# An AdaLN block of gated scan, SwiGLU and routed experts: a new order of loads and work in the first stage, additions counted from one, and the last shared tile taken out of its banks first

## The reference

```
x = L0_attn_x                                    # 2 x 2048 x 512
h = layernorm(x) * (1 + ca) + sa
q, k, v = split(rms(h) @ w_qkv.T);  q, k = rms(q), rms(k)
w = exp(k)
y = sigmoid(q) * (cumsum(w * v) / (cumsum(w) + 1e-6))
u, g = split(y @ w_swiglu.T)
x = x + ga * (h + u * silu(g) @ w_out.T)
h = layernorm(x) * (1 + cb) + sb
shared = gelu(h @ shared_w1 + shared_b1) @ shared_w2 + shared_b2
routed = sum over the 2 best of 8 experts of gate * (gelu(h @ w1 + b1) @ w2 + b2)
x = x + gb * (routed + shared)
```

## Time and profile before

| | us |
|---|---|
| median of three runs | 2011.24 (2011.04 to 2012.4) |
| the profiled execution, by its own timing | 2010.7 |
| its span in the trace | 2008.9 |
| TensorE busy | 1944.8 (97%) |
| VectorE busy | 1279.0 (64%) |
| ScalarE busy | 646.6 (32%) |
| GpSimd busy | 438.7 (22%) |
| mean granted TensorE clock | 0.987 |

### The profile page before, as it was taken

The page is one execution under the profiler, slowest core; times in us unless marked ns, Lnnn a source line. Parts: engine busy times, 40 slices in busy tenths (PEclk is TensorE's granted clock), DMA queues, the critical chain, the costliest instruction groups (busy, mean ns, idle before and its releaser), DMA issues.

```text
span 2008.9 us, 26671 instructions
## 1 busy us (share of the span) xinstructions
PE 1944.8 (97%) x9106; PEld 1567.2 (78%) x9106; DVE 1279.0 (64%) x2674; ACT 646.6 (32%) x1318; POOL 438.7 (22%) x315
## 2 busy tenths in 40 slices
PE   6999999999999999998999999999999999999996
PEld 4677888888888888886887787777787667688885
DVE  6577777685545555559164465466367686488886
ACT  3545556631111112111112212212223223255553
POOL 0012000040000000017000110110052252458887
PEclk8999999999999999999999999999999999999998
DMA  5124110141011210123111311311235464468888
GB/s 224 58 89 132 51 53 27 48 142 63 24 39 63 74 44 20 63 79 121 65 63 63 107 47 67 123 65 53 96 106 179 130 199 154 146 117 152 154 154 130
DMA packets 86112, 189.99 MB, mean 95 GB/s; under 512 B 10021, under 2 KB 26662, under 8 KB 80940
## 3 DMA queue, kind: packets, MB, share of 16 engines
q1 hardware_dynamic: 63116, 130.98, 19.3%
q0 software_dynamic: 22864, 57.31, 13.8%
HBM read 118.56 MB, written 72.12 MB: 95 GB/s over the span
## 4 chain that ended last, share of the span: by engine, by line
PE 75%; DVE 14%; issue 4%; ACT 4%; DMA 2%; SPq 0%; POOLq 0%; ACTq 0%; DVEq 0%
PE bank L670 11%; PE bank L672 11%; PE bank L671 11%; PE bank L675 8%; PE bank L677 8%; PE bank L676 8%; PE bank L909 3%; PE bank L911 2%; PE bank L896 1%; PE bank L939 1%; PE bank L937 1%; PE bank L938 1%; PE bank L836 1%; PE bank L689 1%; ACT kv_sum L1084 1%
## 5 line engine op out<-in xcount | busy, mean ns | idle before, releaser
L670 PE MATMUL bank<-x_hi,w_blk 128*128 128x512 f32 x1024 | 404.0, 395 | 9.2 <-DVE x_lo L1315 6.3
L672 PE MATMUL bank<-x_hi,w_blk 128*128 128x512 f32 x1024 | 399.9, 390 | 0.0
L671 PE MATMUL bank<-x_lo,w_blk 128*128 128x512 f32 x1024 | 399.4, 390 | 0.0
L1473 DVE TENSOR_TENSOR s_t<-act_t,bank 128x512 f32<-128x512 f32 x128 | 87.8, 686 | 302.9 <-PE bank L672 300.1
L670 PEld LDWEIGHTS bank<-x_hi,w_blk 128*128 128x128 f32 x1024 | 192.9, 188 | 50.1 <-DVE x_lo L1315 7.0
L1134 ACT ACTIVATE s_hi<-s_t 128x512 fp32r<-128x512 f32 x128 | 80.9, 632 | 458.8 <-DVE s_t L1473 436.4
L672 PEld LDWEIGHTS bank<-x_hi,w_blk 128*128 128x128 f32 x1024 | 192.8, 188 | 41.0
L671 PEld LDWEIGHTS bank<-x_lo,w_blk 128*128 128x128 f32 x1024 | 192.9, 188 | 38.8
L547 POOL TENSOR_SCALAR w_blk<-raw 128x1536 fp32r<-128x1536 f32 x16 | 23.8, 1487 | 854.3 <-PE bank L677 694.2
L675 PE MATMUL bank<-w_blk,s_hi 128*128 128x512 f32 x512 | 200.6, 392 | 0.0
L677 PE MATMUL bank<-w_blk,s_lo 128*128 128x512 f32 x512 | 199.3, 389 | 0.0
(11 more groups left out here) (250 smaller groups left out, 3635.8 us busy)
## 6 DMA issues: line engine op xcount, KB each, us to landing
x_t<-y_scratch SPq DMA_DIRECT2D x24, 1024.0 KB
residual<-r_t SPq DMA_DIRECT2D x16, 1024.0 KB, 4.3
r_t<-residual SPq DMA_DIRECT2D x16, 1024.0 KB
raw<-w_swi POOLq DMA_DIRECT2D x12, 768.0 KB, 4.5
y_scratch<-y_t SPq DMA_DIRECT2D x32, 256.0 KB, 2.7
r_t<-x_tok SPq DMA_DIRECT2D x8, 1024.0 KB
h_rows<-hrow SPq DMA_DIRECT2D x32, 256.0 KB
y_scratch<-hT SPq DMA_DIRECT2D x8, 1024.0 KB, 3.9
```

The source lines that it names most:

```text
L670: nc.tensor.matmul(dst, w[:, 0, col:col + P], rhs_hi, start=start, stop=False)
L671: nc.tensor.matmul(dst, w[:, 0, col:col + P], rhs_lo, start=False, stop=False)
L672: return nc.tensor.matmul(dst, w[:, 1, col:col + P], rhs_hi, start=False, stop=stop)
L1473: nc.vector.tensor_tensor(s_t[:, s % 2, :], act_t[:, s % 2, :], bank[4 + (2 * s + 1) % 3][:, :], ALU.mult).then_inc(f.s_ok, 1)
```

## The change

It has four parts.

First stage, start. SyncE's loads are put in a new order: the modulation weights first, then the 128 rows of group 0 alone (`x0_in`), then `w_qkv` in three column parts (k, q, v of all rows, 1 MB each) with the other rows of x after the first. The weights are split by halves of such a part (`part_of`, six halves), and `project(0, k)` waits for its halves. The modulation products of the second sequence move behind `project(0, 1)` and `project(1, 0)`, and `c_b` to another address. Group 0's norm is cut into its two halves, and the shift comes from the bank. `columns_lo(1)` moves ahead of `norm(2)`, and group 0 is taken out of the loop. The scalar engine's table is loaded before it waits for c.

First stage, square roots. The shift and three Newton steps become a seed by logarithm and exponential on the scalar engine (`seed_spread`, `seed_root`) and one Newton step on the vector engine (`one_step`).

First stage, running sum of w. The four products with the triangle become four transposes, and the vector engine sums along the columns with four scans of 128 columns each.

The end. The tables of `slots_of_experts` are loaded by GpSimd after the first stage and count 16 on each of the four semaphores of the additions, so all counts of additions begin at one, and `max` with 16 becomes `add` of 16. The last shared tile is multiplied into four free rows, two of them ahead of slot 0's first step (`last_shared`), which releases the banks by `left`; its additions to `r_t` come later (`last_residual`).

```diff
@@ SyncE
             sp.dma_start(c_t[:, :], c).then_inc(c_in, 16)
-            sp.dma_start(xr[:, 0:NSUB, :], rows_of(0, NSUB)).then_inc(xa_in, 16)
             load_wmod(0)
             load_wmod(1)
+            sp.dma_start(xr[:, 0:1, :], rows_of(0)).then_inc(x0_in, 16)
             for dst, src in ((ident_t, ident), (tri_t, tri)):
                 sp.dma_start(dst[:, :], src).then_inc(turn_in, 16)
-            for i in range(B0):
-                piece(i)
+
+            load_part(0)
+            sp.dma_start(xr[:, 1:NSUB, :], rows_of(1, NSUB - 1)).then_inc(xa_in, 16)
+            load_part(1)
+            load_part(2)
             load_wmod(2)
...
                 if j >= NA:
-                    sp.wait_ge(sc_st[j % NA], 16 * (j // NA))
+                    sp.wait_ge(sc_st[j % NA], 16 * (j // NA + 1))
                 sp.sem_inc(sc_go)
@@ GpSimd
+            pool.wait_ge(y_st, 16 * NG)
+            for k, (dst, src) in enumerate(((thr_t, thr), (jota_t, jota), (jcol, jcol_in))):
+                pool.dma_start(dst[:, :], src).then_inc(sc_st[k], 16)
+            pool.dma_start(steps_t[:, :, :], steps.rearrange("p (k e) -> p k e", k=2)).then_inc(sc_st[3], 16)
@@ TensorE
                 for m in range(NC):
-                    if i == 0:
-                        pe.wait_ge(w_ok, m + 1)
+                    if g == 0 and m % 2 == 0:
+                        pe.wait_ge(part_ok, 2 * k + m // 2 + 1)
...
                 for m in range(NC):
                     at_ = slice(m * P, (m + 1) * P)
-                    ins = nc.tensor.matmul(bank_w[:, at_], w_t[g % 2][:, at_], tri_t[:, :], start=True, stop=True)
+                    ins = nc.tensor.transpose(bank_w[:, at_], w_t[g % 2][:, at_], ident_t[:, :])
...
             for g in range(NG):
                 project(g, 0)
+                if g == 1:
+
+                    pe.wait_ge(gain_ok, 1)
+                    modulate(bank[0][:, :], 1, same_rows(1))
                 if 0 < g and g + 1 < NG:
                     turn_group(g + 1)
                 project(g, 1)
                 if g == 0:
+                    modulate(bank[2][:, :], 0, same_rows(1))
+                    project(g, 2)
                     turn_group(1)
+                    continue
                 if g == 1:
                     pe.wait_ge(gain_ok, NB_SEQ)
+                    pe.wait_ge(shift_ok, NB_SEQ)
...
-                    pe.wait_ge(ffn["s"].ev_ok, NSUB * LAST + j + 1)
+                    pe.wait_ge(left, j + 1)
...
-                    pe.wait_ge(ffn["s"].ev_ok, NSUB * LAST + j + 3)
+                    pe.wait_ge(left, j + 3)
@@ ScalarE
+            def seed_spread(t, first=0, end=NSUB):
+
+                act.wait_ge(a.va_ok, t + 1 if (t, first) == (0, 0) else t + 2)
+                then(nc.scalar.activation(sv_a[:, 0, first:end], va_a[:, t % 2, first:end], ACT.Ln))
+                nc.scalar.activation(sv_a[:, 0, first:end], sv_a[:, 0, first:end], ACT.Exp, scale=-0.5).then_inc(a.sv_ok, 1)
...
             for g in range(NG):
                 square(g, 0)
                 if g + 1 < NG:
                     columns_hi(g + 1)
+                if g == 0:
+                    for n in range(1, NSUB):
+                        square_h(n)
+                    seed_root(0)
+                if g == 1:
+                    take_shift(1)
 
                 t, n = g // NSUB + 1, g % NSUB
+                if t < NT and n == 0 and g > 0:
+                    seed_spread(t)
                 if t < NT and n in (1, 2):
                     square_h(NSUB * t + 2 * n - 2)
                     square_h(NSUB * t + 2 * n - 1)
+                    if n == 2:
+                        seed_root(t)
@@ VectorE
+            def one_step(dst, seed_, of):
+
+                step = sqv[:, 0:dst.shape[1]]
+                then(nc.vector.tensor_tensor(step, seed_, seed_, ALU.mult))
+                then(nc.vector.scalar_tensor_tensor(out=step, in0=step, scalar=-0.5, in1=of, op0=ALU.mult, op1=ALU.mult))
+                then(nc.vector.scalar_tensor_tensor(out=dst, in0=step, scalar=1.5, in1=seed_, op0=ALU.add, op1=ALU.mult))
...
-                if g % G_SEQ == 0:
-                    then(nc.vector.tensor_scalar(W_t[g % 2][:, :], bank[0][:, :], W_EPS, None, ALU.add))
-                else:
-                    sum_before = in_chunks(W_t[(g - 1) % 2])[:, :, P - 1:P].broadcast_to([P, NC, P])
-                    then(nc.vector.tensor_tensor(in_chunks(W_t[g % 2]), in_chunks(bank[0]), sum_before, ALU.add))
+
+                for m in range(NC):
+                    at_ = slice(m * P, (m + 1) * P)
+                    from_ = W_EPS if g % G_SEQ == 0 else W_t[(g - 1) % 2][:, (m + 1) * P - 1:(m + 1) * P]
+                    ins = nc.vector.tensor_tensor_scan(W_t[g % 2][:, at_], bank[0][:, at_], tri_t[:, :], from_, ALU.add,
+                                                       ALU.bypass)
+                then(ins)
...
                     elif n < 3:
+                        if n == 1:
+                            spread(t)
                         norm(NSUB * t + 2 * n - 2)
...
-                nc.vector.tensor_scalar(due_t[:, :, :], due_t[:, :, :], 16, None, ALU.max).then_inc(due_ok, 1)
+                nc.vector.tensor_scalar(due_t[:, :, :], due_t[:, :, :], 16, None, ALU.add).then_inc(due_ok, 1)
...
+            def last_shared(g):
+
+                nc.vector.tensor_tensor(late_rows[g][:, :], bank[g][:, :], gbs_t[1][:, :], ALU.mult).then_inc(left, 1)
...
-            dve.wait_ge(ffn["s"].ev_ok, NSUB * NT)
-            slot_u(0, expert(0))
+            e_0, e_1 = expert(0), expert(1)
+            dve.wait_ge(ffn["s"].dn, NB_S * NT)
+            last_shared(0)
+            last_shared(1)
+            slot_u(0, e_0)
             slot_x(2)
-            slot_u(1, expert(1))
+            last_shared(2)
+            last_shared(3)
+            slot_u(1, e_1)
+            dve.wait_ge(r_in, 16 * 3 * NT)
+            last_residual(0)
             slot_g(0)
+            for g in range(1, NSUB):
+                last_residual(g)
```

More of the change, by code:

```diff
@@ L287, in piece_of @@
         def piece_of(i):
-            if i < B0:
-                return w_qkv[i], w_blk[:, 1 + i, 0, :], w_blk[:, 1 + i, 1, :], SWI_W
             if i < S0:
@@ L1462, in _ @@
                 scales(g)
[L1463 to L1464 removed]
+                denominator(g - 1)
             k_times_v(NG - 1)
```

176 lines of the change are left out of this document (107 added, 69 removed).

## The result

The changed kernel takes 1993.55 us, the median of four runs (1990.65 to 1998.55), where the kernel before, on the same chip, takes 2011.14 (2010.27 to 2012.4): a ratio of 0.9915, with a 95% interval of 0.9896 to 0.9934. The forecast was 1995.0, with 1988 to 2004 as its range.

What follows compares the result with a forecast made beforehand. First stage bound by a ring of DVE and ACT steps, not by TensorE at 97%; start and end also lose time. -5.6 - 3.5 - 0.4 + 0.7 - 7.3 - 0.1 = -16.2, giving 1995.0 on the median's scale; range 1988 to 2004.

Steps and rivals of the forecast that it cites:

- Start: First stage's start: first running sum at 45.4 against 50.98, -5.6 us; -3 if TensorE falls to half clock there.
- Rival C: The start doesn't follow, as shift and seeds are in series on ACT and the clock falls: 1999 to 2000; 8%.
- Body: First stage, from the first running sum to that of group 30: 350.2 us, forecast as -3.5.
- The held steps: First-stage DVE steps held by GpSimd's four splits, each for the rest of 3.5 us; six groups: 69.2 to 74.1.
- the ring: First stage's loop of dependent DVE and ACT steps sets the pace: 44.4 us per four groups, 45.4 before.
- Scans: First stage's running sum of w on DVE: 128-column scans 0.39 us apart, costing 0.4 us per four groups.
- rivals A, D and E: A: scans 0.475 apart, 2002, 12%. D: seeds hidden, scans 0.29, 1990, 10%. E: scans over 0.56 us, slower, 6%.
- `denominator(31)`: At stage b's start, this DVE step lies between GpSimd's splits and adds +0.7 us (0 to 1).
- Additions from one: Kernel's end: additions 1 to 4 no longer wait for landing, so addition 70 follows `o_t(70)`: -7.3 us.
- Rival B: The end doesn't follow: waits for landing return in another form and the store holds `o_t`: 2000; 8%.
- Last shared tile: Before the slots: TensorE's turn no longer waits, but `slot_o(0)` waits for the tile's store: -0.1 us, -1 to +1.
- Rival F: First stage: twelve transposes per group pull TensorE's clock to 1.2 GHz, some 60 us in all: 2050; 1%.

## Why the prediction was right, step by step

Start: forecast -5.6, measured -6.4 and, with the start alone, -5.2. The steps came where the lists put them: the first product at 6.26 (7.2), `project(0,0)` at 18.42 (18.8), `project(1,0)` at 32.17 (32.8), `project(1,1)` at 40.23 (40.5), behind w as said. The loads were a little quicker than 2.5 us per MB. Rival C fell, but a part of it shows: over the thirteen profiles with this start the gain is 3.9 to 6.8 us. In the two with the least, `project(0,0)` begins at 19.52, as in the kernel with the start alone (19.47, first running sum 45.81), and 3.4 us at 1.2 GHz cost 1.2 to 1.3 us more. That is the forecast's case of half clock, in which it had -3.

Body: forecast 350.2, measured 349.95. The mechanism is shown by the two kernels with one engine made heavier. The intervals of `quotient` were forecast at 12.2, 12.1, 9.8 and 10.4, measured at 12.06, 12.03, 9.70 and 10.10. The sum is partly luck: by segments the forecast was 57.1, 74.1, 177.5, 41.6, and the trace has 56.9, 77.4, 174.3, 41.4. The held steps cost 3.3 more than forecast and the sixteen groups behind them 3.2 less; of these 2.0 are the ring (43.9 for 44.4 per four groups), and the rest is TensorE making up for the wait ahead of them. The saving came out as 4.8 and not 3.5, since I took the difference between two followed lists, of which that for the kernel before was 1.0 too short.

Scans: forecast 0.39 apart, measured 0.383; rivals A, D and E fell with it. (The forecast's lower value of 0.29 leaves out the start column and the overlap that it counts in the other two; with them it would be 0.26. Nothing hung on it.) At 403 ns with a constant start and 463 with a column, they bear out that `tensor_tensor_scan` runs at half throughput (the Trainium skill, "DVE: opcode table, instruction layouts, handler registers and perf-mode slots", section "Datapath and trigger behaviour"): a product of 512 columns takes 691 ns, 1.04 ns per column, and the scan with a constant start, less the 0.16 of a short instruction, 1.9.

What I did not say plainly is that the third part of the change was worth nothing by itself: the forecast gives one number for square roots and scans together. The lists, followed for each alone, gave +3.4 for the scans and -7.7 for the square roots; the kernels gave 0 and -2.0 of the stage. Both are off by 3 to 6 us in the same segment, that of the held steps. Which step meets a split depends on when weights land and on what runs ahead of it: the changed kernel's code took 346.45 to 349.95 in four profiles. My four fixed windows of GpSimd could not give that.

`denominator(31)`: forecast +0.7, measured +0.1 at most: the second tile of stage b begins 34.38 us after the last running sum before and 34.47 in the changed kernel.

Additions from one: forecast -7.3, measured -6.6 in the trace, and 5.9 (7.29 less 1.35) and some 7.5 us of time when undone. The mechanism holds: SyncE's waits for landing were the cause. The size was off since addition 70 was put at the end of `o_t(70)`; the last slots come 1.8 to 1.9 us apart, and GpSimd still issues addition 69 until 1981.24. Rival B fell.

Last shared tile: forecast -0.1, measured +0.35 in the first profile and +3.2 in the second. The step that failed is the cost of the late additions to `r_t`: I let them end 3.8 us later than before. The last one ended 6.8 later, as two of them were held by GpSimd's splits, which I had named for the first stage and for `slot_o(0)` but not there. The time of the kernel without this part does not tell a difference, so the loss is shown by the timelines only, though by all of them.

Clock: it did not fall by the transposes. Rival F fell: 200 to 300 us of the changed kernel, with twelve transposes per group, and the kernel with sixteen run at full clock outside the waits of the held steps. The Trainium skill ("TensorE: Matmul & The Clock Gate", section "Part 4: PE-mode transpose") would have had them count for less; no run here shows it.

What the forecast did not have: 2.85 us between the last running sum and the slots, of which 1.7 go with the clock of single executions.

So the mechanisms of the start, the ring, the scans and the additions hold, and the last shared tile is the part that it had wrong. That the median went down by 17.6 where the sum said 16.2 is closer than the terms: start and body gave 2.1 more than forecast, the additions and the last tile 1.2 less, and the profile has the 2.85 besides.

## What to carry to other kernels

An engine at 97% need not be the bound: look whether the other engines' waits in a steady stretch ever name it, and test by making one engine's list heavier at a time. When a ring of two others sets the pace, find the wait inside it and put work that is due anyway into that wait; only then does an edit that spares the busy engine pay (0.1 us before, 11.6 after).

A step of two columns can cost as much as the longest instruction that GpSimd runs beside it. Cut GpSimd's long instructions, or move either of the two; a faster list may just meet them at a worse moment. And where a profile and a median differ by some us, read the clock by stretch before a cause is sought in the code.

## What the runs showed of the hardware

A step of DVE with two inputs in SBUF, held by GpSimd, goes on between two of GpSimd's instructions: cut to 256 columns (0.7 us each), they hold it for 0.60 and 0.66 us, where one of 1536 columns held it for 3.28. GpSimd pays for it with 4.2 us for the six, once 5.55, in place of 3.4 to 3.5. The copy ahead of the subtraction, with one input, holds DVE's step as well (1.33 and 1.21 us).

A transpose of 128 x 128 in float32 is one instruction where the product is two, and takes 0.11 us of TensorE: four in 0.44, the triangle's four products in 0.89.

GpSimd issues a gather and an addition every 3.2 us when nothing holds it (12.8 us for four), and two additions without a gather between them every 1.9 to 2.1.
